# Three Swin blocks on one core: softmax over keys on partitions, scores made twice, dense products in four 64x64 parts

## The reference, cut to what matters

```
xn  = layernorm(x) * g1 + b1                       # over the 48 channels
win = windows of 7x7 pixels of (rolled) xn         # 2048 windows of 49 tokens
q, k, v = split(win @ qkv_w + qkv_b)               # 6 heads of 8 channels
s   = q @ k^T / sqrt(8) + rel_bias[head] (+ mask)  # 49 x 49 per window and head
out = softmax(s) @ v ; out = out @ proj_w + proj_b
x   = x + out (rolled back)
x   = x + gelu(layernorm(x)*g2 + b2 @ w1 + c1) @ w2 + c2    # hidden 192
```

## Time and profile before

| | |
|---|---|
| median of 3 runs | 8296.84 us |
| the profiled execution | 8299.7 us, its span 8298.0 us |
| TensorE busy | 7781.9 us, 94% |
| VectorE busy | 6095.1 us, 73% |
| ScalarE busy | 6242.5 us, 75% |
| GpSimd busy | 3585.1 us, 43% |
| mean granted TensorE clock | 0.976 |

### The profile page before, as it was taken

One profiled execution on the slowest core, in us unless ns is written; L12 is line 12 of the kernel. 1 busy time (PEld: TensorE's weight loads), 2 busy tenths in 40 slices (PEclk: granted clock), 3 DMA queues, 4 the chain that ended last, 5 costly groups with the idle time before them and its releaser, 6 DMA issues.

```text
span 8298.0 us, 213285 instructions
## 1 busy us (share of the span) xinstructions
PE 7781.9 (94%) x76732; PEld 4632.0 (56%) x76732; DVE 6095.1 (73%) x12339; ACT 6242.5 (75%) x11905; POOL 3585.1 (43%) x2453
## 2 busy tenths in 40 slices
PE   6899999999999999999999999999999999999997
PEld 4655555555555555555555555555555555555554
DVE  6377777777777777777777777777777777777774
ACT  0288878887888888778878878888787888787781
POOL 4244444444444444444444444444444444444440
PEclk9999999999999999999999999999999999999996
DMA  7000000000000000000000000000000000000006
GB/s 218 9 20 20 19 19 19 19 21 19 19 19 19 21 18 19 19 20 19 19 19 20 19 19 19 19 20 19 21 19 19 19 21 19 19 19 21 19 16 205
DMA packets 286131, 236.84 MB, mean 29 GB/s; under 512 B 41564, under 2 KB 280670, under 8 KB 284766
## 3 DMA queue, kind: packets, MB, share of 16 engines
q1 hardware_dynamic: 240944, 179.42, 8.1%
q10 hardware_dynamic: 35886, 19.97, 0.8%
q0 software_dynamic: 8192, 22.49, 0.8%
HBM read 112.56 MB, written 109.18 MB: 27 GB/s over the span
## 4 chain that ended last, share of the span: by engine, by line
issue 53%; POOL 30%; PE 10%; ACT 3%; DMA 3%; DVE 1%; POOLq 1%; SPq 0%; ACTq 0%; DVEq 0%
POOL E L411 19%; POOL Kbd L420 11%; PE bank L867 1%; PE bank L900 1%; DMA cm<-xT 1%; DMA xT<-cm 1%; PE bank L885 1%; PE bank L926 1%; PE bank L957 1%; PE bank L848 1%; PE bank L849 1%; PE bank L1017 1%; PE bank L943 1%; ACT E L472 0%; PE bank L962 0%
## 5 line engine op out<-in xcount | busy, mean ns | idle before, releaser
L411 POOL TENSOR_TENSOR E<-E,rs 113x588 f32<-113x588 f32 x1536 | 1819.2, 1184 | 3379.0 <-DVE rs L701 3379.0
L670 DVE TENSOR_TENSOR S<-bank,bias 113x294 f32<-113x294 f32 x3072 | 1412.5, 460 | 1428.9 <-PE bank L885 1364.8
L420 POOL TENSOR_TENSOR Kbd<-KT,headmask 112x1176 f32<-112x1176 f32 x768 | 1701.8, 2216 | 1042.6 <-ACT KT L478 1042.6
L867 PE MATMUL bank<-ident,E 113*113 113x113 f32 x9216 | 1620.3, 285 | 289.1 <-ACT ET L446 160.4
L867 PEld LDWEIGHTS bank<-ident,E 113*113 113x113 f32 x9216 | 1232.6, 180 | 1086.5 <-issue 540.8
L446 ACT ACTIVATE ET<-bank 113x339 f32<-113x339 f32 x3072 | 1367.7, 445 | 489.2 <-PE bank L867 471.3
L900 PEld LDWEIGHTS bank<-ET,V 113*48 113x48 f32 x36864 | 1005.5, 126 | 781.5 <-ACT ET L446 485.5
L695 DVE TENSOR_REDUCE sm<-E 113x12 f32<-113x588 f32 x1536 | 1163.8, 758 | 328.2 <-ACT E L472 328.2
L678 DVE TENSOR_REDUCE mx<-S 113x12 f32<-113x588 f32 x1536 | 1172.2, 763 | 39.6
L684 DVE TENSOR_TENSOR S<-S,mx 113x588 f32<-113x588 f32 x1536 | 1168.5, 761 | 0.0
L900 PE MATMUL bank<-ET,V 113*48 113x49 f32 x36864 | 1152.5, 212 | 10.3 <-issue 9.8
(11 more groups left out here) (88 smaller groups left out, 9136.9 us busy)
## 6 DMA issues: line engine op xcount, KB each, us to landing
xin<-xT SPq DMA_DIRECT2D x384, 98.0 KB, 2.0
xT<-xout SPq DMA_DIRECT2D x384, 98.0 KB, 1.8
xin<-xT SPq DMA_DIRECT2D x384, 73.5 KB, 2.0
xT<-xout SPq DMA_DIRECT2D x384, 73.5 KB, 1.8
xT<-cm POOLq DMA_DIRECT2D x128, 171.5 KB, 3.6
cm<-xT SPq DMA_DIRECT2D x128, 171.5 KB, 3.6
tm<-in_x SPq DMA_DIRECT2D x128, 147.0 KB
out<-tm ACTq DMA_DIRECT2D x128, 147.0 KB
```

The source lines that it names most:

```text
L411: pool.tensor_tensor(e, e, r, ALU.mult).then_inc(norm_done, 1)
L420: pool.tensor_tensor(Kbd[:, j.mod(2), p0:p0 + P // 2], k, m, ALU.mult).then_inc(kbd_done, 1)
L670: dve.tensor_tensor(strided(S[:, p, 0, 0:1], [[1, HN]]), pS[p % 2][0:M2, 0:HN], bi, ALU.add)\
L867: last = pe.transpose(pT[0:M2, k * M2:(k + 1) * M2], strided(E[:, j.mod(2), p, 2 * k, 0:1], [[1, M2]]), ident[0:M2, 0:M2])
```

## The change

Keys now stand on partitions. KT (keys, 24 channels of 3 heads on each of four groups of 32 partitions) is the stationary operand for the second scores; their transpose is never needed, since exp of them is already the moving operand of the product with V. The maxima over keys are needed per query, which now lies along the columns. So scores are made twice. `scores1` makes them with queries on partitions (from Qt and the spread Kbd); VectorE reads the maxima straight from PSUM; one product with the identity (`maxima_across`) lays them along columns, VectorE copies them to mxT, and four DMAs (`spread_max`) write them as a 25th row into the spread Qbd. The 25th row of KT holds -1, so `scores2` contracts over 25 rows and comes out less the maxima. Both scores, 147 columns each in a bank, accumulate onto the bias, which `begin_scores` writes by one fp32r product of 296 columns for each of four banks (the bias is stacked as a rounded part and a rest). A group is two windows of two images; there are four groups a step. `exps` reads PSUM and waits for the maxima of the same group too, since both lie in the same banks.

V carries ones in spare columns, so that the product with V also gives the sums. The whole product of a step (96 products of 49 columns in 64x32 parts) runs at the start of an iteration. The sums are spread by four DMAs (`spread_sums`), inverted by Ln and Exp on ScalarE, and GpSimd multiplies the 392 columns once (`normalize`). GpSimd also spreads Q. ScalarE's evacuations of K, Q, V and the output go to VectorE. Projection and first residual move from step d to e. Dense products are four parts of 64x64 with 196 columns. The centering is folded into the weights of q, k, v and w1, so the normalised input is xin or x1 times the inverse deviation. The one-hot products are made for both directions, and the waits of many groups sit on a `nop` ahead of them (`ready`).

```diff
 @block.sync
+            def spread_max(j, half):
+                sp.wait_ge(mxT_done, gv(j, 2, half + 1))
+                n = 2 * HP
+                for q in range(4):
+                    to = strided(Qbd[32 * q + HC:32 * q + HC + 1, j.mod(2), 2 * half, 0, 0, 0:1],
+                                 [[2 * N, n], [N, 2], [1, N]])
+                    of = strided(mxT[n * q:n * q + n, half, 0:1], [[HI, 2], [1, N]])
+                    sp.dma_start(to, of).then_inc(mxd_in[half], 16)
+            def spread_sums(j):
+                sp.wait_ge(oS_done, gv(j, 1, 1))
+                for q in range(4):
+                    ...
+                    sp.dma_start(sums[32 * q:32 * q + HC, :], of).then_inc(sums_in, 16)
             def iteration(a, b, c, d, e):
+                if d: spread_sums(d)
+                if c: spread_max(c, 1)
                 load(a.next().next())
+                if b: spread_max(b, 0)
                 if e: store(e)
 @block.gpsimd
+            def iteration(a, b, c, d, e):
+                if b: spread_q(b, 0); spread_q(b, 1)
+                if d: normalize(d)
+                if a: spread_k(a, 0); spread_k(a, 1)
 @block.scalar
+            def exps(j, k, b):
+                act.wait_ge(s2_mm, gv(j, 4, k + 1))
+                if b:
+                    act.wait_ge(mx_done, gv(b, 4, k + 1))
+                e = strided(E[:, k, 0, 0, 0:1], [[WN, 4], [1, WN]])
+                s = strided(pS[0:M2, 0, S2:S2 + 1], [[512, 4], [1, WN]])
+                act.activation(e, s, ACT.Exp).then_inc(exp_done, 1)
+            def inverse_sums(j):
+                act.wait_ge(sums_in, gv(j, 64, 64))
+                act.activation(lo[:, :], sums[:, :], ACT.Ln).then_inc(lo_done, 1)
+                act.wait_ge(lo_done, gv(j, 1, 1))
+                act.activation(rb[:, :], lo[:, :], ACT.Exp, scale=-1.0).then_inc(rb_done, 1)
+            def iteration(a, b, c, d, e):       # each if its step exists
+                exps(c, 0, b); square(a, ...); square(e, ...); exps(c, 1, b)
+                inverse_std(a, ...); inverse_std(e, ...); inverse_sums(d); exps(c, 2, b)
+                hidden(e, 0); hidden(e, 1)
+                act.preload_act_table_set("natural_log_exp_and_others")
+                exps(c, 3, b)
 @block.vector
+            def iteration(a, b, c, d, e):       # each if its step exists
+                evac_o(d, c); evac_mx(c, 1); maxima(b, 0, c); residual1(e); maxima(b, 1, c)
+                normal1(a); normal2(e); maxima(b, 2, c); evac_k(a); evac_q(a)
+                evac_mx(b, 0); maxima(b, 3, c); evac_v(a); residual2(e)
 @block.tensor
+            def maxima_across(j, half):
+                pe.wait_ge(mx_done, gv(j, 4, 2 * half + 2))
+                mm(pA[:, 0, MT:MT + M2], mx[:, MXC * half:MXC * half + 128], ident[0:M2, 0:M2], ...)
+            def begin_scores(b, c, d, k):
+                wait kbd_done(b), mxd_in[k // 2](c), exp_done(c, k) or exp_done(d, 4)
+                for q in range(4):
+                    mm(pS[:, q, S1:S1 + 2 * SW], stackr[:, :], rows, start=True, stop=False)
+            def scores1(j, k, c):
+                for q in range(4):
+                    for i in range(2):
+                        mm(pS[HI * i:HI * i + N, q, S1:S1 + WN], Qt[32 * q:32 * q + HC, j.mod(2), k, i, :],
+                           Kbd[32 * q:32 * q + HC, ...], start=False, stop=not c)
+            def scores2(j, k):                  # KT rows 0 to 24 against Qbd rows 0 to 24
+                ...
+            def values(j):
+                pe.wait_ge(exp_done, gv(j, 4, 4)); ready()
+                for k in range(J):
+                    for h in range(HP):
+                        for i in range(2):
+                            for q in range(4):
+                                mm(pA[32 * q:32 * q + 32, i, N * k:N * (k + 1)],
+                                   V3[HI * i:HI * i + N, ...], E[HI * i:HI * i + N, k, q, h, :], ...)
+            def iteration(a, b, c, d, e):
+                wait v_done(b); values(d); maxima_across(c, 1)
+                for k in range(J):
+                    if k == 2: wait va1_done(a); maxima_across(b, 0)
+                    begin_scores(b, c, d, k); scores1(b, k, c); scores2(c, k)
+                    if k == 0: project(e); center1(a, c, d); center2(e)
+                    if k == 1: var1(a); var2(e)
+                    if k == 2: up(e); query_key(a); up_c(e)
+                    if k == 3: value(a, b); down_ab(e); down_c(e)
```

More of the change, by code:

```diff
@@ L33 @@
 HP = HEADS // 2
-VC = HP * C
+HC = HP * D
+J = P // 2
+HT = TOK // 2
+RQ = 128
+WN = HP * N
+SW = WN + 1
+MXC = 4 * 2 * HP
 class Step:
@@ L636, in _ @@
+                    chain(last)
             dve.wait_ge(bias_mm, NPH)
@@ L703, in normal1, with evac_o @@
+            def evac_o(j, c):
+                if c:
+                    dve.wait_ge(mxt_mm, gv(c, 2, 2))
+                else:
+                    dve.wait_ge(pv_mm, gv(j, 1, 1))
+                if not j.before(1):
+                    dve.wait_ge(oT_done, gv(j, 1, 0))
+                dve.tensor_copy(oS[:, :, :], pA[0:RQ, :, 0:HT]).then_inc(oS_done, 1)
             def normal1(j):
@@ new lines, in iteration @@
+                if d:
+                    evac_o(d, c)
+                if c:
+                    evac_mx(c, 1)
+                if b:
+                    maxima(b, 0, c)
+                if e:
+                    residual1(e)
+                if b:
+                    maxima(b, 1, c)
+                if a:
+                    normal1(a)
+                if e:
+                    normal2(e)
+                if b:
+                    maxima(b, 2, c)
+                if a:
+                    evac_k(a)
+                    evac_q(a)
@@ L803, in _ @@
+                if b:
+                    evac_mx(b, 0)
+                    maxima(b, 3, c)
+                if a:
+                    evac_v(a)
+                if e:
+                    residual2(e)
             sweep(dve, iteration)
@@ new lines, in centered, with summed @@
+            def centered(to, x):
+                for i in range(2):
+                    r = HI * i
+                    for half in range(2):
+                        last = mm(to[HI * half:HI * half + HI, i, 0:HT], center[r:r + C, r:r + HI],
+                                  x[r:r + C, HT * half:HT * half + HT], start=True, stop=True)
+                return last
+            def summed(to, x):
+                for half in range(2):
+                    r = HI * half
+                    for i in range(2):
+                        last = mm(to[HI * i:HI * i + HI, half, 0:HT], ones[r:r + C, r:r + HI],
+                                  x[r:r + C, i, :], start=True, stop=True)
+                return last
@@ L939, in center2 @@
+                last.then_inc(proj_mm, 1)
             def center2(j):
                 pe.wait_ge(x1_done, gv(j, 1, 1))
[L941 to L944 removed]
+                ready()
+                centered(pB, x1[:, j.mod(2)].rearrange("p r c -> p (r c)")).then_inc(ctr2_mm, 1)
             def var2(j):
@@ new lines, in up, with up_c @@
+                for i in range(2):
+                    r = HI * i
+                    for c in range(2):
+                        last = mm(pB[HI * c:HI * c + HI, i, 0:TOK], w1[r:r + C, t, HI * c:HI * c + HI], xn2[r:r + C, :],
+                                  start=True, stop=True)
+                last.then_inc(fc1_mm, 1)
+            def up_c(j):
+                t = j.t
+                pe.wait_ge(gelu_done, gv(j, 2, 1))
+                ready()
+                for i in range(2):
+                    r = HI * i
+                    for half in range(2):
+                        last = mm(pB[HI * half:HI * half + HI, i, 0:HT], w1[r:r + C, t, 128:HID],
+                                  xn2[r:r + C, HT * half:HT * half + HT], start=True, stop=True)
+                last.then_inc(fc1_mm, 1)
@@ L971, in iteration @@
                     if c:
-                        transposes(c, p)
-                    if b and p % 2 == 0:
-                        scores(b, p)
-                    if p == 1:
+                        scores2(c, k)
+                    if k == 0:
+                        if e:
+                            project(e)
                         if a:
-                            center1(a)
+                            center1(a, c, d)
+                        if e:
+                            center2(e)
```

791 lines of the change are left out of this document (409 added, 382 removed).

## The result

The changed kernel takes 10991.3 us (median of 4 runs, 10987.1 to 10999.8) against 8296.9 (4 runs, 8291.6 to 8301.7): ratio 1.3245, 95% interval 1.3227 to 1.3262. It is 2694 us slower, and 2807 above the forecast of 8184.

What follows compares the result with a forecast made beforehand. TensorE, busy 94%, was taken as the bound. Chain 18.72 plus 0.60 for the loop's jump plus 0.25 for clock falls gave step 19.57 against 20.20; 8299.7 - 243 + 130 = 8187, so 8184 us; range 7750 to 9100.

Steps and rivals of the forecast that it cites:

- Set-up +130: Ahead of the loop: one-hot products made twice +103, bias tiles +17, folding center into the weights +10; together +130 us.
- Full-clock chain 18.72: One step in program order from V's start until the next V may start: 18.72 us against 19.67 before.
- rival 1: Small products do not run eight abreast; four abreast gives chain 21.1, step 21.95, 9100 us; chance 0.25 with fp32r.
- Term (a), V: Product with V, 24 rounds of eight parts: 1.50 us taken, 1.25 by rate per round, 4.3 per instruction.
- Term (d): DMAs, 8 for maxima and 4 for sums, 0.41 us an issue: all hidden with 2.5 us to spare.
- I add 0.25 for such falls: Clock falls from TensorE idling 2.3 us in each step near 13: 0.25 us a step.
- Rival 2: Clock low as TensorE streams only 70% of the step: half the time 9400 us, always 10,900; chance 0.14.
- Residual2 spaced 18.5 to 19: Sign of being right: the second residual add, once a step, spaced 18.5 to 19 us in ordinary steps.
- granted clock below 0.9: Sign of being wrong, for rival 2: granted clock below 0.9 over the loop.
- No wait of TensorE on a DMA: Sign of being right: TensorE never waits on a DMA.
- ScalarE at 11: Sign of being right: ScalarE's work at 11 us a step, from an estimated sum of 11.2.
- theory G: From the follow-ups, not the forecast: single TensorE pauses above about 1 us can drop the clock; unbroken work restores it.

Runs made afterwards that it cites:

- c_order: Against the changed kernel: product with V in two halves, up_c behind group 3's scores and value, first norm's Ln ahead of group 1's exp; 9828 us.
- c_nofill16: c_un16 without its five dense products; 9634 us.
- c_un16: c_order with five dense products, results never read, one in each of five TensorE pauses, and loops of 16 steps instead of 8; 9477 us.
- e_v48: Changed kernel with V's product in half the instructions at the same columns, 96 a step instead of 192; 886 us faster.
- e_sp: Changed kernel with SyncE sending the second half's maxima ahead of the sums; gained 61 us.
- e_fill: Changed kernel with eleven dense products, results never read, in TensorE's gaps of each step; time inside the band 12,100 to 12,900 us.
- c_dense: c_order with five dense products in its pauses and four more between up and query_key; cost 830 us.
- c_upc: Product with V in two halves as in c_order, plus up_c behind group 3's scores and value; time stayed, intervals overlapping the split V alone.

## Why the prediction was wrong

By its own steps:

- Set-up +130: right (first residual at 530.0, for 528).
- Full-clock chain 18.72: those of its parts that can be read stand. Its products were reckoned at 1.67 ns a column, which no row ahead of it shows; the timeline of before has it, as two products of 392 columns start 0.66 us apart, 1.68 ns a column (median 657 ns of 384 such pairs):

```profile
4010.00 0.82 PE L918 MATMUL bank<-xn,wq 112*112 112x392 f32 x2
4010.66 0.82 PE L919 MATMUL bank<-xn,wk 112*112 112x392 f32 x2
```

  A four-part product of 196 columns, forecast at 0.33 us, takes 0.33 in the kernels that show it at full clock (query-key in c_order, from start to start, median 332 ns). For a change of division the forecast has 0.16; here the second scores start 0.29 us after the first, and the projection, in another division, 0.39 after the second, so 0.10. The 0.16 for a tail and the 0.05 for a semaphore are shown by no run one by one. Maxima take 0.77 for 0.82: of the 0.06 added to 763 ns for PSUM, 8 ns are there (771, L711). In the timeline above, scores of both kinds together take 0.75 us with their tail; fp32r bias 0.79 for four, also with tail; from the end of group 0's scores to the end of center2 2.24 us (forecast 2.27); the Ln wait of 1.35 is there, and GELU's ahead of up_c. Sixteen instructions of scores start 0.29 us before the next sixteen, for 0.26 forecast and 0.49 at four abreast, so they run eight abreast. That the bias takes 0.125 us a product was an assumption that no row showed; four of them start 0.72 us before what follows, change of division included, for the 0.66 of the forecast. So four abreast is out, and so is a bias at twice the forecast's price, the form of rival 1 that its chance of 0.25 counts as "with fp32r". The sum itself was never measured. In c_nofill16 66 steps lie wholly at full clock, and their median is 19.6 us, with V's rest pause in it but with up_c moved and the Ln early, which should have made the chain shorter still; in c_un16, with 1.8 us of fill, 211 such steps have a median of 19.8. The kernel before had 19.67. So even at full clock no version here with such steps gained more than 0.1 us a step on it in the median.
- Term (a), V: 1.50 forecast, bounds 1.25 to 4.3. Rate and filling were not far off (96 instructions in 1.10, so 192 near 1.9 with the tail); the group takes 3.5 on average, with the pause in it. I bounded the cost of an instruction, never asked whether 192 pairs would arrive in time. Worth 2.0 us a step; in e_v48 V's group was 1.9 us shorter and the step 2.3 (26.9 to 24.6).
- Term (d), "all hidden with 2.5 us to spare": wrong. The issue takes 0.75 us (median), not 0.41, the eight around this place stand in line, and the maxima miss their time by 0.7 us at full clock. Mis-sized and small: a wait of 0.7 us a step, of which mending it alone (e_sp) returned 0.16.
- "I add 0.25 for such falls": this is the step that failed. I had 2.3 us of idle ahead of up_c, 1.5 ahead of group 2, and the earlier trace rows in which the clock fell after such stretches. I took each fall for an exception, as that of the loop's jump had been (2.78 us at "issue", then 0.50) in a kernel busy for 94%. Here it falls in nearly every step, 391 times, and stays low for 17 us on average (6.8 at the old jump), in the step shown through group 2, up, query-key, group 3 and value. As an estimate from the trace of the changed kernel, TensorE's groups are together 6.6 us a step longer, without V, than at full clock, of which about 1.3 is taken back by the wait ahead of up_c (1.12 for 2.4): 5.3 us a step, where I had 0.25. (The "1.2 GHz" of the forecast's sum is the granted clock of 0.50; no run shows a frequency. That TensorE's terms double there is nearly so: query-key's 0.33 us is 0.65 at 0.50, start to start in c_order, and four bias products that start 0.72 us ahead of the scores at full clock start 1.28 ahead at 0.50.) Then 18.72 + 0.60 + 2.0 + 0.7 + 5.3 is 27.3, for 26.9 measured; I take the rest for slack that the terms share.
- Rival 2 was the right one with a chance of 0.14, and it stopped at half the time low (9400) or always (10,900); the share was 0.65, and V's pause, which it did not have, lengthened the step besides. It did little to the clock: with the pause nearly gone (e_v48) the share is still 0.60, with 390 falls. That 10,900 lies so near the measured 10,991 is partly luck, since it has neither V's pause nor the DMA wait, and the low level in every part of the step instead of two thirds of it. The range's end of 9100 left out a mechanism whose two falls stood in the rows.
- "Residual2 spaced 18.5 to 19", "granted clock below 0.9": 26.4 and 0.69. "No wait of TensorE on a DMA": there is one. ScalarE at 11: 10.6.

Less idle time went with a smaller share at the low level from c_nofill16 to c_un16 (3.0 and 1.6 us a step, share 0.53 and 0.32). But in e_fill's 12 us window TensorE was busy throughout, by the profile, and the clock stayed at 0.50.

What stays open: what brings the clock down and back, beyond the pauses, since c_dense, c_upc and e_fill did not answer as theory G had it; and how V's 192 small instructions could be fed without a pause. A kernel with the pauses gone and the clock always full was not reached.

## What to carry over

Before a change that takes TensorE from nearly full to two thirds full, price the whole step at a granted clock of 0.50 as well, and take every pause like those here (0.7 to 2.8 us) as a possible fall of the clock, not as idle time that costs nothing: here a chain 1 us shorter on paper became a step 6.7 us longer. Count the instructions of a step, not only their durations: 192 small products in one place stood at "issue" for over 0.4 us in 272 of 384 steps here, 96 with the same columns in 42. And if pauses can't be removed, short dense products placed exactly in them can pay (157 us in c_un16); more of them than the pauses hold cost 663 to 1387 us here.

## What the runs showed that was not expected

- A packet of 16,384 bytes of the kind "instruction" took 1.07 us (median of 1541), and in nine of ten pauses inside V TensorE went on 1.2 to 1.6 us after the end of one.
- Eight 32-row parts run abreast in the scores (16 instructions in 0.49 us, the next 16 start 0.29 us after their start), and 49x32 parts at 11.5 ns each (96 in 1.10 us).
- A DMA of the maxima, 2.3 KB, holds SyncE's queue 0.75 us (median; 735 to 1314 ns), one of the sums, 36.8 KB, 0.76 (697 to 1418).
- The loop with 16 steps gained 252 us over 8, the one with 32 another 60, within its interval.
- The low level lasts far longer than the pauses: the mean low stretch is 17 us in the changed kernel and 36 in c_order, where no mean idle time is over 6 us a step.
